# A two-layer transformer chain in one call: bias and attention in one block, semaphores counted from zero, bit-linear work shared with GpSimd

## The reference, cut to what matters

```python
x = x + 0.5 * ffn(ln(x))                 # signs of the weights, 256 -> 1024 -> 256, exact gelu
x = x + local_and_latent_attention(ln(x))
x = x + 0.5 * ffn(ln(x))
x = x + 0.5 * bit_linear(ln(x))
x = x + relative_attention(ln(x))
x = x + 0.5 * bit_linear(ln(x))

def bit_linear(x):                        # a layer norm of its own, gain ln_gamma, offset ln_beta
    w_q = clip(round(weight / (mean(|weight|) + 1e-5)), -1, 1)
    gamma = max(|xn|)                     # one maximum over all tokens
    xq = clip(xn * 128 / gamma, -128 + 1e-5, 128 - 1e-5)
    return (xq @ w_q) * gamma * mean(|weight|) / 128

def relative_attention(x):                # 16 heads of 16 features, buckets of distance from -31 to 31
    q, k, v = split(x @ w_qkv.T);  q = q / 4
    attn = q @ k.T + take(q @ rk, bucket) + take(k / 4 @ rq, bucket)
    p = softmax(attn)
    out = p @ v + (p summed by bucket) @ rv
    return out @ w_proj.T + b_proj
```

## Time and profile before

| | |
|---|---|
| Runs | 2425.19, 2425.92, 2429.5 us; median 2425.92 |
| Profiled execution | 2436.6 us, span 2434.7, mean granted TensorE clock 0.924 |
| TensorE (products) | 2030.2 us busy, 83% |
| VectorE | 1617.5 us, 66% |
| ScalarE | 1234.3 us, 51% |
| GpSimd | 493.8 us, 20% |
| Moved | 195.13 MB |

### The profile page before, as it was taken

The page is one execution under the profiler, slowest core; times in us unless marked ns, Lnnn a source line. Parts: engine busy times, 40 slices in busy tenths (PEclk is TensorE's granted clock), DMA queues, the critical chain, the costliest instruction groups (busy, mean ns, idle before and its releaser), DMA issues. The chain is left out here.

```text
span 2434.7 us, 74675 instructions
## 1 busy us (share of the span) xinstructions
PE 2030.2 (83%) x32204; PEld 1285.8 (53%) x32280; DVE 1617.5 (66%) x2553; ACT 1234.3 (51%) x1862; POOL 493.8 (20%) x794
## 2 busy tenths in 40 slices
PE   3986887888887796497773999999999999999975
PEld 2654555556455564354673555555555555555544
DVE  6775354453533677774353888888888888888847
ACT  3761221223212575322330677767777777777754
POOL 0002000000000000000001554444543454435410
PEclk7998999998989898698886899999999999999996
DMA  3001000000000000133237555544555455545412
GB/s 106 1 1 43 3 1 19 2 19 3 1 19 2 1 1 5 25 122 114 105 149 244 148 139 135 137 123 118 135 136 136 131 138 134 132 125 135 110 31 74
DMA packets 273793, 195.13 MB, mean 80 GB/s; under 512 B 206744, under 2 KB 260310, under 8 KB 273210
## 3 DMA queue, kind: packets, MB, share of 16 engines
q1 hardware_dynamic: 262586, 139.27, 22.5%
q0 software_dynamic: 10496, 50.75, 5.5%
q10 hardware_dynamic: 384, 0.33, 0.1%
HBM read 91.69 MB, written 93.88 MB: 76 GB/s over the span
## 5 line engine op out<-in xcount | busy, mean ns | idle before, releaser
L2020 DVE TENSOR_REDUCE a1c_nm<-a1c_S 128x1 f32<-128x1024 f32 x512 | 609.6, 1218 | 98.9 <-PE a1c_S L2105 98.3
L1960 ACT ACTIVATE a1c_PT<-a1c_ST 128x1024 f32<-128x1024 f32 x499 | 510.3, 1023 | 57.5 <-PE a1c_ST L2105 54.7
L1975 ACT ACTIVATE a1c_Pb<-a1c_S,a1c_nm 128x192 f32<-128x192 f32 (+1 forms) x512 | 212.9, 416 | 217.7 <-DVE a1c_nm L2020 216.7
L1904 POOL TENSOR_TENSOR a1c_lt<-a1c_lt 128x256 f32<-128x256 f32 (+5 forms) x448 | 254.7, 568 | 35.4
L2010 DVE COPY a1c_PbT<-a1c_T 96x512 f32<-96x512 f32 x256 | 175.7, 686 | 96.1 <-PE a1c_T L2137 93.7
L2105 PE MATMUL a1c_S<-a1c_KR,a1c_Q 54*32 54x512 f16 (+13 forms) x2816 | 180.7, 316 | 19.7 <-DMA a1c_Gx<-a_bias 18.3
L2105 PE MATMUL a1c_ST<-a1c_Q,a1c_KR 57*128 57x256 f16 (+2 forms) x1066 | 175.0, 284 | 22.3 <-ACT a1c_PT L1960 21.5
L2105 PE MATMUL a1c_S<-a1c_KL,a1c_Q 54*32 54x512 f16 (+11 forms) x3136 | 191.8, 323 | 0.6 <-ACT a1c_Pb L1975 0.3
L2105 PE MATMUL a1c_S<-a1c_Gx,ident 64*32 64x96 f32 (+2 forms) x4352 | 184.8, 240 | 0.0
L1896 POOL DMA_DIRECT2D a_band<-a1c_Pb x128 | 71.4, 558 | 495.6 <-ACT a1c_Pb L1975 495.3
L2137 PE MATMUL a1c_T<-ident,a1c_Pb 128*96 128x128 f32 x1024 | 168.1, 288 | 0.8 <-DVE a1c_mhl L2034 0.8
(11 more groups left out here) (344 smaller groups left out, 4138.4 us busy)
## 6 DMA issues: line engine op xcount, KB each, us to landing
a_band<-a1c_Pb POOLq DMA_DIRECT2D x128, 384.0 KB, 3.3
a_bias<-a1b_G SPq DMA_DIRECT2D x32, 768.0 KB, 8.1
a1c_Gx<-a_bias SPq DMA_DIRECT2D x128, 192.0 KB, 4.3
a1c_Dt<-a_band SPq DMA_DIRECT2D x128, 126.0 KB, 3.7
a1c_Q<-a_qk SPq DMA_DIRECT2D x192, 64.0 KB
a1c_Vw<-a_values SPq DMA_DIRECT2D x64, 102.0 KB, 2.8
a1c_KL<-a_qk SPq DMA_DIRECT2D x96, 64.0 KB
a1c_KR<-a_qk SPq DMA_DIRECT2D x90, 64.0 KB
```

The costliest lines, as they stand in the source:

```text
L1904: add = lambda o, x, y: nc.gpsimd.tensor_tensor(o, x, y, ALU.add)
L1960: nc.scalar.activation(PT[:, q % 8, :, :], place(q), ACT.Exp).then_inc(s["exp"], 1)
L1975: nc.scalar.activation(Pb[:, band_slot(I, c), w0:w1], SP[:, t % 2, I * P - 32 + w0:I * P - 32 + w1], ACT.Exp, bias=nm[:, t // 16 % 2, col: ...
L2020: nc.vector.tensor_reduce(nm[:, t // 16 % 2, col:col + 1], SP[:, t % 2, :], AX.X, ALU.max, negate=True).then_inc(s["max"], 1)
```

## The change

**Semaphores.** They start from zero: `arm`, `ONE` and every `ONE +` in a wait are gone. There is no block of clears between phases. `turn_over` hands the names of the finished phase to `G.old`, and the next phase's SyncE program clears them (`clear_old`): first of all in the feed-forward and attention phases, behind the first loads in the others. A block at the very end clears the last phase's names.

**Bias and attention in one block.** `rel_bias` becomes a class `Bias` with one method for each engine, called at the head of the attention block's programs. Queries 0 and queries 2 now run alone, before the keys of their unit, over the banks of `pq` and `pk` in turn, and their copies are shared by ScalarE (two) and VectorE (two). The order is queries 0; keys 0 with queries 1; keys 1; queries 2; keys 2 with queries 3; keys 3. Loads of the attention part need only wait for the last query step or for the stores that they read. SyncE stores units 0 to 2, loads queries, keys and the first bias rows (units 0 and 1 hold heads 0 to 7), and then stores unit 3 (`last_out`). The tiles of the attention part are placed in another order in SBUF, so that those filled early don't lie over tiles in use.

**Bit-linear.** GpSimd normalises every other tile. ScalarE makes the high part straight from the unscaled tile with the scale in the same instruction; VectorE scales and clips from above into a tile of its own (`x1`), and clips from below within the low part's instruction. ScalarE takes the scaled product out of PSUM (`ys`), and GpSimd adds it to `x`, for all but the last group, which VectorE does as before. The output scale is computed behind the first group.

```diff
-def arm(sp, s):
-    for x in s.values():
-        sp.sem_inc(x, ONE)
+def sems(nc, G, prefix, names):
+
+    s = {n: nc.alloc_semaphore(f"{prefix}_{n}") for n in names.split()}
+    G.live.extend(s.values())
+    return s
+
+
+def clear_old(G, sp):
+
+    for x in G.old:
+        sp.sem_clear(x)
+
+
+def turn_over(nc, G):
+
+    for x in G.old:
+        nc.release_semaphore(x)
+    G.old, G.live = G.live, []
+
-    def clear():
-        with nc.Block() as block:
-            @block.sync
-            def _(sp):
-                for x in s.values():
-                    sp.sem_clear(x)
...
 def bit_phase(nc, G, A, r, out=None):
...
+        def normalise(eng, on, i, k, done):
+            for t in range(k, CT, 2):
+                g = i * CT + t
+                on.tensor_scalar(xn[:, i % 2, t, :], G.x[:, g, :], G.mv[:, g, 0:1], scl[:, g:g + 1],
+                                 ALU.subtract, ALU.mult).then_inc(done, 1)
...
         def _(pool):
+            pool.wait_ge(s["scl"], 2)
+            for i in range(NC):
+                if i >= 2:
+                    pool.wait_ge(s["xT"], (i - 1) * KD)
+                normalise(pool, nc.gpsimd, i, 1, s["xnp"])
+                if i == 1:
+                    pool.wait_ge(s["wsum"], 1)
+                    nc.gpsimd.partition_all_reduce(wall[:, :], wsum[:, :], P, bass.bass_isa.ReduceOp.add).then_inc(s["wall"], 1)
+            pool.wait_ge(s["max1"], 1)
+            nc.gpsimd.partition_all_reduce(gall[:, :], pmax[:, :], P, bass.bass_isa.ReduceOp.max).then_inc(s["gmax"], 1)
+            for i in range(NC - 1):
+                rows = G.x[:, i * CT:(i + 1) * CT, :]
+                pool.wait_ge(s["ys"], i + 1)
+                nc.gpsimd.tensor_tensor(rows, ys[:, i % 2, :, :], rows, ALU.add).then_inc(s["out"], 1)
...
-            act.wait_ge(s["gdve"], 4)
             for i in range(NC + 1):
                 if i < NC:
-                    nc.scalar.activation(xT[:, i, :, :], xT[:, i, :, :], ACT.Copy, scale=gi[:, :]).then_inc(s["scaled"], 1)
-                if i >= 1:
-                    act.wait_ge(s["xq"], i)
-                    if i >= 3:
-                        act.wait_ge(s["Y"], i - 2)
-                    nc.scalar.activation(xhi[:, (i - 1) % 2, :, :], xT[:, i - 1, :, :], ACT.Copy).then_inc(s["xhi"], 1)
+                    if i >= 2:
+                        act.wait_ge(s["Y"], i - 1)
+                    nc.scalar.activation(xhi[:, i % 2, :, :], xT[:, i, :, :], ACT.Copy, scale=gi[:, :]).then_inc(s["xhi"], 1)
+                if i == 1:
+                    act.wait_ge(s["gdve"], 4)
+                if i >= 2:
+                    act.wait_ge(s["Y"], i - 1)
+                    if i >= 4:
+                        act.wait_ge(s["out"], i - 3)
+                    nc.scalar.activation(ys[:, i % 2, :, :], psY[:, i % 2, :, :], ACT.Copy, scale=osc[:, :]).then_inc(s["ys"], 1)
...
             def clip(i):
-                dve.wait_ge(s["scaled"], i + 1)
-                nc.vector.tensor_scalar(xT[:, i, :, :], xT[:, i, :, :], CLIP, -CLIP, ALU.min,
-                                        ALU.max).then_inc(s["xq"], 1)
+                if i >= 2:
+                    dve.wait_ge(s["xlo"], i - 1)
+                nc.vector.tensor_scalar(x1[:, i % 2, :, :], xT[:, i, :, :], gi[:, :], CLIP, ALU.mult,
+                                        ALU.min).then_inc(s["xq"], 1)
 
             def low_part(i):
+                dve.wait_ge(s["xq"], i + 1)
+                dve.wait_ge(s["xhi"], i + 1)
+                if i >= 2:
+                    dve.wait_ge(s["Y"], i - 1)
+                nc.vector.scalar_tensor_tensor(xlo[:, i % 2, :, :], x1[:, i % 2, :, :], -CLIP, xhi[:, i % 2, :, :],
+                                               ALU.max, ALU.subtract).then_inc(s["xlo"], 1)
+
+            def out_scale():
+                step(dve, nc.vector.tensor_tensor(osc[:, :], gall[:, :], wall[:, :], ALU.mult), g)
+                step(dve, nc.vector.tensor_scalar(osc[:, :], osc[:, :], 0.5 / QB, None, ALU.mult), g)
+
+            def residual():
+                rows = G.x[:, (NC - 1) * CT:, :]
+                dve.wait_ge(s["Y"], NC)
+                nc.vector.scalar_tensor_tensor(rows, psY[:, (NC - 1) % 2, :, :], osc[:, :], rows, ALU.mult,
+                                               ALU.add).then_inc(s["out_v"], 1)
...
+                if i < NC:
+                    clip(i)
+                    low_part(i)
+                if i == 0:
+                    out_scale()
+                if i == NC:
+                    residual()
...
-def rel_bias(nc, QH, QL, KH, KL, tabs, GD):
+class Bias:
...
+    def alone(self, u):
+        return u % 2 == 0
...
+    def banks(self, u, st):
+        return self.pk if self.alone(u) and st % 2 == 1 else self.pq
...
+    def store(self, sp, u):
+        m, half = divmod(u, 2)
+        if u >= 2:
+            self.wait_out(sp, u - 2)
+        sp.wait_ge(self.s["kev"], self.NK * (u + 1))
+        for h in range(8):
+            sp.dma_start(self.GD[8 * m + h, :, :].rearrange("(p r) x -> p r x", r=32)[:, self.R * half:self.R * half + self.R, :],
+                         self.Gt[:, u % 2, h, :, :]).then_inc(self.s[f"out{u % 2}"], 16)
+
+    def sync(self, sp):
+        for u in range(self.NU - 1):
+            self.store(sp, u)
...
+        for u in range(self.NU):
+            if u >= 2:
+                self.wait_out(act, u - 2)
+            for st in range(self.NQ):
+                act.wait_ge(self.s["q"], u * self.NQ + st + 1)
+                for j in range(2 if self.alone(u) else 4):
+                    out, src = self.copy_place(u, st, j)
...
+        def copies(u):
+            if u >= 2:
+                self.wait_out(dve, u - 2)
+            for st in range(self.NQ):
+                dve.wait_ge(self.s["q"], u * self.NQ + st + 1)
+                for j in (2, 3):
+                    out, src = self.copy_place(u, st, j)
+                    self.nc.vector.tensor_copy(out, src).then_inc(self.s["qdv"], 1)
+
+        for u in range(self.NU):
+            if self.alone(u):
+                copies(u)
+            a, d = self.copied(u + 1, 0)
+            dve.wait_ge(self.s["qev"], a)
+            dve.wait_ge(self.s["qdv"], d)
+            for x in range(self.NK):
+                dve.wait_ge(self.s["k"], u * self.NK + x + 1)
+                g = self.Gt[:, u % 2, :, :, self.KX * x:self.KX * x + self.KX]
+                self.nc.vector.tensor_tensor(g, self.pk[:, x % 4, :].rearrange("p (x h r) -> p h r x", x=self.KX, h=8), g,
+                                             ALU.add).then_inc(self.s["kev"], 1)
...
+        for u in range(self.NU):
+            if self.alone(u):
+                for st in range(NQ):
+                    by_query(u, st)
+            for i in range(NQ):
+                for x in range(3):
+                    by_key(u, 3 * i + x)
+                if u + 1 < self.NU and not self.alone(u + 1):
+                    by_query(u + 1, i)
...
 def rel_attend(...):
         def _(sp):
-            arm(sp, {n: x for n, x in s.items() if n not in ("pw0", "pw1", "k0_in")})
+            clear_old(G, sp)
+            bias.sync(sp)
...
+            bias.wait_queries(sp)
             load_queries(0, 0)
             load_keys(0)
             sp.wait_ge(s["zero"], 1)
+            bias.wait_out(sp, 0)
+            bias.wait_out(sp, 1)
             load_bias(0, 0)
             load_queries(0, 1)
             load_bias(0, 1)
+            bias.last_out(sp)
+            bias.wait_out(sp, 2)
             load_values(0)
             load_windows(0, 0)
+            bias.wait_out(sp, 3)
+            sp.dma_start(bp[:, :], A["b_proj"].partition_broadcast(P)).then_inc(s["bp_in"], 16)
             load_keys(1)
...
```

More of the change, by code:

```diff
@@ L20, with __init__ @@
 CW = CT * P
[L23 removed]
 class Count:
[L29 to L30 removed]
+    def __init__(self, sem, base=0):
+        self.sem, self.k = sem, base
     def value(self):
[L33 removed]
+        return self.k
 def step(eng, ins, c):
@@ L205, in ffn_phase @@
         psY = ps("psY", [P, 2, CT, D])
-        s = sems(nc, ctx, f"ffn{r}", "eps sd rstd xn xT xhi xlo xb H h hhi hlo Y scaled out sums stat")
+        s = sems(nc, G, f"ffn{r}", "eps sd rstd xn xT xhi xlo xb H h hhi hlo Y scaled out sums stat")
         block = ctx.enter_context(nc.Block())
@@ L1883, in _ @@
                                ).then_inc(s["k0_in"], 16)
+            bias.wait_sums(pool)
+            nc.gpsimd.memset(Gx[:, :, 8, :], 0.0).then_inc(s["zero"], 1)
             nc.gpsimd.memset(Pb[:, 0:4, 0:32], 0.0).then_inc(s["zero"], 1)
@@ L1940, in _ @@
         def _(act):
+            bias.scalar(act)
+            bias.wait_queries(act)
             for g in range(2):
@@ L2002, in _ @@
         def _(dve):
+            bias.vector(dve)
             def band_out(d):
```

826 lines of the change are left out of this document (408 added, 418 removed).

## The result

The changed kernel takes 2403.7 us (median of 4 runs, 2393.58 to 2405.32) against 2427.7 for the kernel before (4 runs): ratio 0.9891, 95% interval 0.986 to 0.9922. The forecast was 2357, with a range from 2338 to 2375. The time fell, as forecast, but by about a third of what was expected.

A forecast was written before the change was run, and what follows sets the result against it. The prediction saw movable time in bias-stage store waits, the joint to attention and semaphore clears between stages. Gains of 18.5 + 52.0 less 1.7 lost in bit-linear made 68.8 us: 2436.6 to 2367.8, at the median 2357, range 2338 to 2375.

The forecast's parts named there:

- Bit-linear, first half: Normalising loop of both bit-linear stages: giving GpSimd half of a normalising pass gains 4.8 us (0 to 6).
- GpSimd's pass fits into the wait for the maximum.: Bit-linear normalising loop: GpSimd's normalising runs within the existing wait for the maximum; no duration given.
- Second half: Bit-linear stages: GpSimd's additions hold VectorE's clip and low part; 6.5 us lost in the second stage, 0 in the first.
- the 0: First bit-linear stage, second half: GpSimd's additions hide under VectorE's statistics, 41.1 us against 41.0, so nothing lost.
- the 0.4: Second bit-linear stage: 0.4 us taken off for the output scale moved behind the first tile.
- Semaphores: Opening, joints between stages and projection: raises dropped and clears moved into the next phase gain 18.5 us (16 to 21).
- Bias stage and joint: Bias stage gains 32.7 us with one store wait of 3.6; joint to attention gains 28.6, leaving 8.0.
- Given back in attention: Start of attention: SyncE's last store and loads delay the shift rows, so the first product by keys loses 9.3 us.
- From the profile to the median: Whole kernel: the profiled run's 10.7 us above the median carried over, turning 2367.8 into 2357 us.
- Free add: Rival, bit-linear stages: low part not held by GpSimd's additions, clip hardly; 16.4 us more gained, 2341 us; chance 0.18.
- A clock lost in the attention loop: Rival, attention loop: TensorE's clock drops after the 9.3 us stand-still, giving 2430 us and up; chance 0.02.

The follow-up runs named there:

- one_switch: The changed kernel with both of GpSimd's all-reduces behind its last normalising pass and VectorE's weight quantising behind the inverse scale; 2382.9 us.
- norm_dve: The changed kernel with all normalising on VectorE, GpSimd keeping the all-reduces and additions; 2375.3 us.
- sem_only: The kernel before with only the semaphore change: start from zero, clears inside the next phase; 2413.8 us, ratio 0.992.
- shift_first: The changed kernel with GpSimd only at its all-reduces, and first shift rows issued ahead of the second group's keys, queries and window; 2364.0 us.
- store_act: The changed kernel with GpSimd only at its all-reduces, and the last bias unit's stores issued by ScalarE, not SyncE; 2359.3 us.
- keys_last: The changed kernel with GpSimd only at its all-reduces, second group's keys and queries loaded behind first shift rows, bias rows and diagonals; 2360.4 us.

## Why the prediction was wrong

- **The step that failed** is "Bit-linear, first half", and in it one sentence: "GpSimd's pass fits into the wait for the maximum." It fails twice. The duration of the pass was never taken from a row. I set GpSimd's half equal to what VectorE was relieved of, and it was 1.24 us a pass and not 0.34. This cost little (one_switch, 30.3 and 30.5), but the 4.8 us that the sharing was to gain did not come in any run: with all passes on VectorE the first halves are 29.3 and 29.5. Worse, I listed what the change adds to GpSimd and not what this does to the instructions it already had there: two all-reduces, now between passes of another kind. One_switch and norm_dve show that this and hardly the pace made it +26.6 in place of -4.8: 5.70 us to get to the all-reduce and 6.97 back stood in the loop of each stage. That is 31.4 of the 35.5 us by which the profile missed its sum.
- **How much of it could be read beforehand**: that GpSimd has two all-reduces in this stage, the first in the middle of the loop to be shared, and that no row had a normalising pass of GpSimd. Its MODIFY_POOL_CONFIG stands 6.7 us ahead of the all-reduce in the trace of before, but VectorE's sum, which the all-reduce waits for, fills that time up to 0.14 us. So the trace allowed for a way in of up to 6.7 us and did not show one, and the way back of 6.97 stood nowhere.
- **Second half**: the mechanism was right, the size off: +10.2 for +6.5. In the second stage 5.8 for 6.5; in the first 4.4 for 0. There the term at fault is the 0: the statistics are not held and cover part of an addition, but three low parts were held all the same. Two sizes of the prediction are also off by its own working: with nothing held the second stage gains 28.6 - 25 = 3.6, or 4.0 with the 0.4, and not 4.3, and four times 0.68 is 2.7 and not 2.4. The mean of 1.81 us for the held normalisings, from which the hold was read, mixes one of 5.33 and seven of 1.26 to 1.38.
- **Semaphores**: right, 17.6 at the opening and the joints and 0.6 in the projection of the changed kernel, and 19.9 in sem_only, for 18.5.
- **Bias stage and joint**: right, 60.2 for 61.3, with one store waited for, though 8.0 us and not 3.6. Two errors cancel: the stage gained 34.5 for 32.7 (148.5 to 114.1 us), the way from its end to the first score product 25.8 for 28.6 (10.8 us left, not 8.0).
- **Given back in attention**: the mechanism right (SyncE's queue, first product by keys 39.9 us after the first score product for 29.7 before), 10.2 for 9.3. Against the second profile of before row 40 is 10.7 late, so hardly anything else is lost. What I had put down to the shift rows alone is the whole queue, with the landing that it waits for: shift_first moved the wait to the diagonals, and only store_act and keys_last brought row 40 clearly down (72.5 and 75.9).
- **From the profile to the median**: I took the profiled run's 10.7 us above the median as a constant of profiling. It was one long run, 9 us of it in the local stage if the second profile is the measure. The changed kernel's profiled run lies on its median. So the miss of 46.7 us in the median is 35.5 of the sum, 10.7 of this, and 0.5 of rounding and of the time around the span.
- **Rivals**: none had a cost of GpSimd's own. "Free add" is refuted by 2.85 and 3.25 us. A clock lost in the attention loop did not come: the granted clock over 860 us of it is 1.00 after as before.

## What to carry to other kernels

Before work is put on an engine that has been nearly idle, look at what it does there already: here some 6 us into an all-reduce and 7 back were paid each time its kinds of work alternated, and they were hidden only as long as the engine had nothing else to do. Such a price may not be readable where it is hidden: when a wait for another engine ends just before the work starts, the trace gives only an upper bound, and a small run of the new order has to measure it. Where a DMA queue is in program order, moving one early load forward moves the wait to the next one in that queue; count all that the queue holds, and what it waits for, up to the last load wanted early. And take stages that the change leaves alone from a second profile before a difference of under 10 us is believed.

## What the hardware showed that was not expected

- GpSimd needs 5.7 to 6.1 us to get to an all-reduce and 7.0 to 7.1 back to normalising passes; two all-reduces in a row took 0.40 and 0.44 (one_switch).
- GpSimd's normalising of 128x256 takes 1.21 to 1.40 us in the changed kernel (from 4.7 ns for a column), its addition of 128x1024 2.35 to 3.3 (from 2.3 ns a column). So the operation with one tile and two scalars for each row as input was the dearer one for each column.
- Beside VectorE's held passes GpSimd's additions stretch too: three in 8.47 us, one in 2.45.
- The same code of 610 us (local attention) took between 603.6 and 619.1 us from run to run. In the two profiles of the kernel before, the longer one shows the lower granted clock, 0.90 and 0.93 for 0.93 and 1.00 in its first 100 us.
